# A fused attention, MLP and convolution kernel: projections in pairs, and image pieces loaded one by one behind two chunks

## The reference, cut to what matters

```python
h = einsum('oc,bchw->bohw', w1, x)                 # 48 -> 288 channels ("expand")
h = relu(_bn(h, g1, b1, m1, v1))
h = conv_general_dilated(h, wd, (1, 1), ((1, 1), (1, 1)), feature_group_count=288)  # depthwise 3x3
h = relu(_bn(h, gd, bd, md, vd))
h = einsum('oc,bchw->bohw', w2, h)                 # 288 -> 48 channels ("project")
return x + _bn(h, g2, b2, m2, v2)
```

## Time and profile before

| | us |
|---|---|
| runs of the kernel before | 2053.95, 2045.63, 2052.09; median 2052.09 |
| the profiled execution's own time | 2046.83 |
| its span, first to last instruction | 2044.9 |
| mean granted TensorE clock | 0.987 |
| busy: PE / PEld | 1939.0 (95%) / 1598.8 (78%) |
| busy: DVE / ACT / POOL | 1447.2 (71%) / 1369.1 (67%) / 648.0 (32%) |

### The profile page before, as it was taken

How to read it: one execution, slowest core, us unless ns; L and a number is a source line. 1 busy time by engine, 2 the same in 40 slices (tenths; PEclk the granted TensorE clock), 3 DMA queues, 4 the chain that set the end, 5 groups by cost and what they waited for, 6 DMA issues and landing times.

```text
span 2044.9 us, 76366 instructions
## 1 busy us (share of the span) xinstructions
PE 1939.0 (95%) x29704; PEld 1598.8 (78%) x29704; DVE 1447.2 (71%) x2586; ACT 1369.1 (67%) x2838; POOL 648.0 (32%) x869
## 2 busy tenths in 40 slices
PE   6999999999999996799999999999999899999998
PEld 4888888888888884455555798888888898888987
DVE  5999999999999995455556556556556556565554
ACT  2787878877778874466666566656656566666655
POOL 4333333333333325013000432525234333425230
PEclk9999999999999997899999999999999999999999
DMA  2222222222222225666554435536263545455341
GB/s 65 72 75 71 75 75 73 75 75 75 75 75 75 75 68 124 150 141 157 136 135 111 102 82 137 100 90 150 72 128 95 114 106 117 87 136 102 98 99 33
DMA packets 286441, 199.46 MB, mean 98 GB/s; under 512 B 225991, under 2 KB 275672, under 8 KB 276488
## 3 DMA queue, kind: packets, MB, share of 16 engines
q1 hardware_dynamic: 282114, 189.12, 37.3%
q0 software_dynamic: 2368, 6.98, 1.9%
q10 hardware_dynamic: 1750, 0.39, 0.1%
HBM read 129.10 MB, written 54.72 MB: 90 GB/s over the span
## 4 chain that ended last, share of the span: by engine, by line
PE 56%; ACT 2%; DMA 1%; issue 1%; DVE 1%; ACTq 0%
PE psum L1091 13%; PE psum L1110 13%; PE psum L1136 10%; PE psum L670 6%; PE psum L655 6%; PE psum L1145 5%; PE psum L644 3%; ACT h2T L1191 1%; DMA room<-tok_mid 1%; DVE h L870 1%; ACT room L736 0%; DVE room L870 0%; ACT room L740 0%; ACTq L722 0%; DMA room<-in_fc_wT 0%
## 5 line engine op out<-in xcount | busy, mean ns | idle before, releaser
L919 POOL TENSOR_TENSOR mats<-mats,dscale 112x2048 f32<-112x2048 f32 x72 | 260.9, 3624 | 455.9 <-DMA mats<-in_taps 453.1
L1091 PE MATMUL psum<-ew,xp 64*100 64x96 f32 x6144 | 318.5, 252 | 24.0 <-DVE h L870 11.2
L1191 ACT ACTIVATE h2T<-psum 96x1024 f32<-96x1024 f32 x192 | 195.9, 1021 | 198.3 <-PE psum L1145 198.3
L870 DVE TENSOR_SCALAR h<-psum 100x384 f32<-100x384 f32 x384 | 212.1, 557 | 155.7 <-PE psum L1091 134.8
L1091 PEld LDWEIGHTS psum<-ew,xp 64*100 64x100 f32 x6144 | 291.3, 165 | 33.6 <-DVE h L870 14.1
L1110 PE MATMUL psum<-h,mats 112*64 112x128 f32 x4608 | 269.3, 276 | 6.6 <-issue 5.0
L1110 PEld LDWEIGHTS psum<-h,mats 112*64 112x64 f32 x4608 | 253.6, 138 | 15.5 <-issue 6.3
L869 ACT ACTIVATE room<-psum 64x512 f32<-64x512 f32 (+1 forms) x384 | 206.6, 538 | 84.6 <-PE psum L1110 78.1
L343 PE MATMUL psum<-kb,qa 128*64 128x256 f32 x2048 | 253.2, 383 | 1.0 <-DVE prob L437 0.5
L870 DVE TENSOR_SCALAR room<-psum 64x512 f32<-64x512 f32 (+1 forms) x288 | 174.2, 605 | 71.7 <-PE psum L1110 65.7
L1136 PE MATMUL psum<-h2T,pw 128*64 128x128 f32 x3072 | 211.1, 280 | 11.3 <-ACT h2T L1191 9.5
(11 more groups left out here) (152 smaller groups left out, 3245.9 us busy)
## 6 DMA issues: line engine op xcount, KB each, us to landing
mats<-in_taps SPq DMA_DIRECT2D x69, 896.0 KB, 6.7
tok_mid<-mid SPq DMA_DIRECT2D x128, 224.0 KB, 1.9
room<-tok_mid SPq DMA_DIRECT2D x64, 448.0 KB, 3.8
piece<-img_mid SPq DMA_DIRECT2D x196, 63.8 KB, 2.4
img_mid<-room SPq DMA_DIRECT2D x128, 97.5 KB, 2.9
kb<-kk SPq DMA_DIRECT2D x512, 24.0 KB
out<-yc SPq DMA_DIRECT2D x32, 384.0 KB, 4.5
scratch<-in_x_tokens SPq DMA_DIRECT2D x126, 96.0 KB, 2.0
```

The costliest lines, as they stand in the source:

```text
L870: return nc.vector.tensor_scalar(dst, src, 0.0, None, ALU.max)
L919: nc.gpsimd.tensor_tensor(m, m, bc(scale[0:MROWS, at:at + TCH], 2, POUT), ALU.mult).then_inc(mats_scaled, 1)
L1091: mm = nc.tensor.matmul(ring[(j + u) % 4][0:PIN, p:4 * CH:4], xp[hx][rows, 2 * j + p, :], w1[rows, c, :], start=True, stop=True)
L1191: nc.scalar.activation(h2T[n % 2][0:CH, :, :], turned_at(n, last)[0:CH, :, 0:POUT * PART], ACT.Copy).then_inc(copied, 1)
```

## The change

1. Projections go in pairs. `projected_at(n)` gives projections 0 and 1 to step 2, 2 and 3 to step 4, 4 and 5 to step 6; 6 and 7 stay in steps 7 and 8. In the last chunk of all nothing changes. PE's `turn(1)`, `turn(3)`, `turn(5)` no longer have a projection ahead of them, so a wait for `copied` is put into the last expansion of steps 1, 3 and 5, ahead of its last quarter (p = 3). DVE adds in the same pairs.
2. SP loads pieces 0..7 of the next half at c = 0 and pieces 8..15 at c = 1. The first piece's second DMA waits until the last matrix load of the chunk has landed, every later piece's second DMA until the piece before it has landed. POOL cuts pieces 0..7 behind the matrices of k mod 3 = 1 and pieces 8..15, with the borders, behind those of k mod 3 = 2.

```diff
+        def pieces_at(c):
+            return range(PR // 2 * c, PR // 2 * (c + 1))
...
+        def projected_at(n):
+            return (NSTEP - 1,) if n == NSTEP else (NSTEP - 2,) if n == NSTEP - 1 else (n - 2, n - 1) if n and n % 2 == 0 else ()
...
-                if k % CHUNKS != 1 or h == HALVES:
+                if k % CHUNKS == 0 or h == HALVES:
                     continue
-                for j in range(PR):
+                for j in pieces_at(k % CHUNKS - 1):
...
                     cut_piece(h % 2, j)
+                if k % CHUNKS == 1:
+                    continue
                 close_borders(pool, h % 2, h)
...
-            def load_half(b, hx, h):
-                for j in range(PR):
+            def load_pieces(b, hx, h, c):
+                k = CHUNKS * (h - 1) + c
+                for j in pieces_at(c):
...
                     for r in range(2):
+                        if r and j > pieces_at(c)[0]:
+                            before = slot_of[j - 1]
+                            sp.wait_ge(piece_loaded[before], 32 * (PER_HALF[before] * (h - 1) + nth_in_slot(j - 1) + 1))
+                        elif r:
+                            sp.wait_ge(mats_loaded[-1], 16 * (k + 1))
...
-                if c == 0 and more(b, hx):
-                    load_half(b + hx, 1 - hx, 2 * b + hx + 1)
+                if c < 2 and more(b, hx):
+                    load_pieces(b + hx, 1 - hx, 2 * b + hx + 1, c)
...
-            def expand(k, c, hx, j):
+            def expand(k, c, hx, j, copies=0):
...
+                        if p == 3 and u == 0:
+                            wait(pe, copied, copies)
...
-                        expand(k + 1, (c + 1) % CHUNKS, (hx + 1) % 2 if c == CHUNKS - 1 else hx, j)
+                        ahead = NSTEP * k + n if n % 2 and n < NSTEP - 1 and j == units_at(n)[-1] else 0
+                        expand(k + 1, (c + 1) % CHUNKS, (hx + 1) % 2 if c == CHUNKS - 1 else hx, j, ahead)
...
-                    if n >= 1:
-                        project(n - 1)
+                    for m in projected_at(n):
+                        project(m)
...
-                    if n >= 1:
-                        add(n - 1, b, hx, c, k)
+                    for m in projected_at(n):
+                        add(m, b, hx, c, k)
```

## The result

The changed kernel takes 2029.88 us (median of 4 runs, 2028.74 to 2033.22), against 2051.68 before on the same chip; the ratio is 0.9919, 95% interval 0.9892 to 0.9946. The forecast was 2036. A second set of 6 runs gave 2030.28 against 2048.05, ratio 0.9905 (0.9876 to 0.9933).

A forecast was written before the change was run, and what follows sets the result against it. PE was taken as the bound. From 2049.6 us, pairs saved 19.3 and their waits cost 6.2, net -13.1; the pieces added 0, giving 2036.5, forecast as 2036 us, range 2023 to 2050.

The forecast's parts named there:

- The pairs' saving: In PE's steps, pairing projections saves 0.28 us a pair if nothing waits: 69 pairs, 19.3 us.
- The wait: PE's new wait for ACT's copy, ahead of the 29th of 32 expand loads, costs 0.09 us each, 6.2 us in all.
- What could be late next on ACT, DVE and the ring: Evacuations, copies, adds and room for two expansions keep up in the new steps; costed at nothing, at most 0.13 a step.
- Part 2 at 0: Moving the piece loads on SP and POOL brings 0 us; bounds for their calmer start -8.4 us to one 3.4 us stall.
- The argument on the chunks with c = 0: PE's stalls there aren't the pieces' doing: a chunk without pieces stalls 3.1 us. Rival blaming pieces: 2028 us, chance 0.15.
- SP is 3 to 4 us late, hidden: At c = 0 SP reaches the next chunk's first matrix load late, but it is wanted some 30 us on; cost 0.
- A chunk misread: The window from 1223.41 was taken as c = 1, its matrices landing near 17 us, ahead of the pieces.
- The borders: POOL's borders, done by 40 us, precede PE's need at 45.5; margin 5 us. Rival that they come late: chance 0.04.
- Turns between queues: DMA engines alternate queues packet by packet, so pieces in SP's queue hold nothing long: moving them brings 0, not 8.4 us.
- The base: Starting time for the whole kernel: 2049.6 us, the mean of all four runs, from which the sum is 2036.5 us.

The follow-up runs named there:

- e3: The changed kernel with the wait for the copy ahead of the last expansion's first quarter instead of its last: 2066.56 us, ratio 1.0078 to the kernel before.
- e5: The changed kernel with the last block's two output stores of each first half issued behind the next chunk's matrices: 2021.49 us, ratio 0.9871 to the kernel before.
- e4: The changed kernel with the wait for the copy one matmul later (u = 1 of p = 3): 2032.8 us, ratio 0.9921 to the kernel before.

## Why the prediction was right

- **The pairs' saving, 0.28 a pair unheld.** Right. Two steps were to take 5.81 + 0.09 = 5.90, and take 5.90. A calm chunk was to fall to 35.8 and is 35.77.
- **The wait, 0.09 each.** Right, and shown from both sides: 1.49 instead of 1.41 in the trace, and e3's 36.7 us for 0.53 more of it (69 x 0.53 = 36.6).
- **What could be late next on ACT, DVE and the ring.** Right at nothing: no new wait stands in the list.
- **Part 2 at 0.** This term was too small. The change is 3 to 8 us faster than the pairs alone. The argument on the chunks with c = 0 held (the stall stays in them, with pieces or without, and e5 cut it by moving the stores), but it looked only there. The pieces' tail into the chunk with c = 1, in which SP's first matrix load waits behind them, had 36.36 us to hide in, where it cost 0.8 us once (k = 16), and lost more of its cover when the pairs shortened the chunk. The step "SP is 3 to 4 us late, hidden" was worked out for the new order, where it is at most 1 us late; the old order, left to itself under faster chunks, is the one that is late, by 4. The tail accounts for 2 to 3 us; where the rest of the 3 to 8 comes from stays open.
- **A chunk misread.** The chunk from 1223.41, whose matrices land in 8.4, has c = 2 and not c = 1 as the prediction says. Nothing hangs on it: in the change the matrices of the chunks with c = 1 have all landed 15 to 17 us behind the chunk's start, and 17 was used.
- **The borders.** Right: no wait at line 1108 is put down to POOL. The pieces took 2.5 us each, and 2.6 were allowed.
- **Turns between queues.** At c = 0 the trace after shows the stall with and without pieces, and e5 shows it shrink from 3.1 to 0.6 us with two stores of 384 KB moved. The Trainium skill's rule (DMA: Bandwidth & Descriptors, section Queues, rings and completion order), that an engine takes turns between its queues packet by packet, agrees with this as to the pieces at c = 0. How stores and matrices together can then hold a packet of code back, by 3.4 us in chunk 21 against e5, no run shows; as to them the measurement decides.
- **The base.** The mean of four runs was used, 2049.6; the measured median before is 2051.68. The forecast gain of 13 stands against 21.8 between medians and 16.6 by the ratio (0.0081 x 2051.68); runs of one kernel spread over 8 us before. That 2036 lies only 6 above the measured 2029.88 is luck in part: from 2051.68 the same sum gives 2038.6, and the 9 us from there down are about the most that the pieces brought, which the forecast had at nothing.

## What to carry to other kernels

Where one engine is the bound and its work alternates between kinds, price a step by start-to-start intervals next to the same work with other neighbours: the differences are the switch costs, and they sum exactly (5.90 forecast and found). A wait put in to make such a grouping legal costs the releaser's end minus the place in the stream, no more (0.09 here, 0.53 more for 12 loads earlier in e3); put it late, up to where it costs next to nothing. And when the bound engine gets faster, look at what ended just in time on the other queues, since a tail that was nearly free becomes the next stall. Where the bound engine stands still and waits for nothing that the profile shows, look for the instruction queue's packets just ahead of the stall's end.

## What the runs showed that was not expected

- Output stores of 384 KB issued 1 us ahead of three loads of 896 KB nearly double the loads' time to landing (6.1 to 11.5 us) and go with a stall of PE of some 3 us, though PE waits for neither: a 16 KB packet of its code starts 17.5 us into the chunk instead of 14.1.
- Gains in PE's calm chunks may not be independent of this: by the medians `LEAD = 2` alone brought 5.4 us, behind the moved stores 16.6 (2021.49 - 2004.91); by the ratios 9.4 and 15.6, which noise could bridge.
- A wait on the matmul of one row half did not stop the loads behind it: one of the next group starts ahead of the held half's last (e4). That they are the other half's is a reading, not a row.
